# Latent attention with a ternary gated feed-forward on one core: fp16 scales from norms, score tiles in pairs

## What is computed

```python
c_kv, c_q = x @ w_dkv, x @ w_dq                       # ranks 64 and 192
k = concat([rope(x @ w_kr), c_kv @ w_uk])             # 16 heads of 64 + 128
q = concat([rope(c_q @ w_qr), c_q @ w_uq])
v = c_kv @ w_uv
out = softmax(q @ k.T / sqrt(192)) @ v @ w_o
x = layernorm(x + out)
x = layernorm(x + (silu(x @ w1q.T) * (x @ w3q.T)) @ w2q.T)   # ternary weights
```

## Time and profile before

| | us |
|---|---|
| median of 3 runs | 1019.66 |
| lowest, highest | 1019.26, 1024.77 |
| the profiled execution | 1020.77 |
| its span, first to last instruction | 1019.1 |
| mean granted TensorE clock | 0.974 |
| attention loops | some 128 to 451 and 608 to 933 |

### The profile page before, as it was taken

How to read it: one execution, slowest core, us unless ns; L and a number is a source line. 1 busy time by engine, 2 the same in 40 slices (tenths; PEclk the granted TensorE clock), 3 DMA queues, 4 the chain that set the end, 5 groups by cost and what they waited for, 6 DMA issues and landing times.

```text
span 1019.1 us, 17708 instructions
## 1 busy us (share of the span) xinstructions
PE 891.6 (87%) x5114; PEld 502.5 (49%) x5114; DVE 681.3 (67%) x1060; ACT 695.9 (68%) x1116; POOL 596.0 (58%) x401
## 2 busy tenths in 40 slices
PE   7888869998999999989889876999999999998985
PEld 3556534444444444448775642444444444444874
DVE  1877747777777777764458674777777777776455
ACT  2733668888888888881333466888888888887132
POOL 0008856767777767772341874776777776777134
PEclk9998979999999999999999897999999999999998
DMA  9734698887778877884510669897878877889301
GB/s 252 231 141 104 148 221 153 149 152 149 145 148 154 153 148 145 146 157 134 180 36 12 132 161 192 148 152 150 153 143 150 154 149 145 151 146 157 120 1 41
DMA packets 420800, 145.34 MB, mean 143 GB/s; under 512 B 405820, under 2 KB 413840, under 8 KB 419728
## 3 DMA queue, kind: packets, MB, share of 16 engines
q1 hardware_dynamic: 419584, 136.88, 67.5%
q10 hardware_dynamic: 592, 5.77, 1.4%
q0 software_dynamic: 576, 2.10, 0.6%
HBM read 23.85 MB, written 7.60 MB: 31 GB/s over the span
## 4 chain that ended last, share of the span: by engine, by line
PE 28%; ACT 25%; issue 20%; DVE 11%; POOL 9%; DMA 3%; ACTq 2%; SPq 1%; POOLq 0%; DVEq 0%
ACT probs L566 11%; ACT P_parts L451 8%; POOL P_parts L398 6%; PE Sb L1103 6%; DVE nmax L825 5%; PE Oa L1132 4%; ACT PT_hi L451 3%; PE Sa L1103 3%; DMA PT_dma<-P_parts 2%; ACT rden_row L451 2%; POOL g_lo L427 1%; DVE qmul L804 1%; PE Sa L1156 1%; PE Sb L1156 1%; DVE Q_parts L795 1%
## 5 line engine op out<-in xcount | busy, mean ns | idle before, releaser
L398 POOL TENSOR_TENSOR P_parts<-probs,P_parts 128x768 f16<-128x768 f32 x256 | 420.8, 1645 | 210.2 <-ACT P_parts L451 210.2
L451 ACT ACTIVATE P_parts<-probs 128x768 f16<-128x768 f32 x256 | 214.3, 838 | 17.0 <-DMA PT_dma<-P_parts 17.0
L566 ACT ACTIVATE probs<-Sa,nmax,limits 128x1024 f32<-128x1024 f32 x128 | 154.0, 1203 | 90.3 <-DVE nmax L828 90.1
L825 DVE TENSOR_REDUCE nmax<-Sb 128x1 f32<-128x1024 f32 x128 | 156.5, 1223 | 55.9 <-PE Sb L1103 55.7
L1103 PE MATMUL Sb<-K_hi,Q_parts 128*128 128x512 f16 x512 | 155.1, 385 | 43.6 <-ACT probs L566 42.8
L1103 PE MATMUL Sa<-K_hi,Q_parts 128*128 128x512 f16 x512 | 156.3, 388 | 34.8 <-ACT probs L566 34.7
L825 DVE TENSOR_REDUCE nmax<-Sa 128x1 f32<-128x1024 f32 x128 | 154.9, 1210 | 29.1 <-PE Sa L1103 29.1
L566 ACT ACTIVATE probs<-Sb,nmax,limits 128x1024 f32<-128x1024 f32 x128 | 154.3, 1205 | 1.5 <-DVE nmax L828 1.5
L1132 PE MATMUL Oa<-PT_dma,V_hi 128*64 128x512 f16 x768 | 132.4, 385 | 0.0
L1103 PEld LDWEIGHTS Sa<-K_hi,Q_parts 128*128 (+1 forms) x512 | 40.1, 99 | 118.7 <-issue 61.2
L371 POOL TENSOR_TENSOR turned<-qmul 128x1024 f32<-128x1024 f32 x16 | 40.1, 2528 | 93.5 <-DVE qmul L804 93.4
(11 more groups left out here) (300 smaller groups left out, 1536.6 us busy)
## 6 DMA issues: line engine op xcount, KB each, us to landing
Q_parts<-turned_parts SPq DMA_DIRECT2D x64, 128.0 KB, 2.4
TT<-ternary SPq DMA_DIRECT2D x2, 2304.0 KB, 9.7
Q_parts<-Q_parts SPq DMA_DIRECT2D x16, 256.0 KB, 2.9
PT_dma<-P_parts SPq DMA_TRANSPOSE x256, 3.6
ternary<-tern ACTq DMA_DIRECT2D x1, 2304.0 KB, 8.2
wo<-in_L_attn_w_o_dram SPq DMA_DIRECT2D x4, 512.0 KB, 8.6
xq<-in_L_attn_x_dram SPq DMA_DIRECT2D x2, 1024.0 KB, 12.1
wq_low<-Wq_lo ACTq DMA_DIRECT2D x1, 2048.0 KB, 12.7
```

The lines of the kernel that those rows point to most:

```text
L398: nc.gpsimd.tensor_tensor(P_parts[:, n % DEEP, 1, :], probs[n % DEEP][:, KP * P:S], P_parts[:, n % DEEP, 0, :], ALU.subtract).then_inc(par ...
L451: return nc.scalar.activation(o, i, ACT.Copy, scale=scale)
L566: nc.scalar.activation(probs[n % DEEP], SS[n % 2][:, :], ACT.Exp, bias=nmax[:, n % 4:n % 4 + 1], scale=score_down, accum_out=den[:, n // 8 ...
L825: nc.vector.tensor_reduce(nmax[:, n % 4:n % 4 + 1], SS[n % 2][:, :], AX.X, ALU.max, negate=True).then_inc(row_max, 1)
```

## The change

Three things are changed together.

**Scales from norms.** The fp16 scales no longer come from maxima of the finished keys and queries, but from bounds: the largest norm of a row of `x` (ScalarE squares eight slices with a running sum; VectorE, TensorE and VectorE take the largest), and maxima and norms of weights. Eleven small steps make the scales (one, a power of -1/2, on POOL), before keys and queries are copied out of PSUM; the scale is applied there, so keys, latent rows and queries are already scaled, and the later products need none. POOL rotates the key and takes its low part. POOL also makes `Wq_lo` of the rotary weights in the setup. SP issues the three stores of ScalarE, for batch 0 behind its loads. TensorE's transposes of `x` wait for `x` alone.

**Values by DMA.** `V_hi` and `V_lo` are DMA transposes of rows 64 to 127 of `K_hi` and `K_lo`. `turn_values`, `values_high` and the `V_lo` subtraction are gone.

**Tiles in pairs.** All four loops step by two tiles. TensorE: scores n + 2 and n + 3, then transposes n and n + 1, the row sums where due, then the values. ScalarE: exponent n + 2, high part of the transposes of n and n + 1, exponent n + 3, high casts n + 2 and n + 3. VectorE: both maxima, then the low part of the transposes. `row_out` moves from ScalarE to VectorE, and the high part of the output from VectorE's second product to a copy on POOL in `low_out`.

The core of the diff:

```diff
+                if b == 0:
+                    sp.wait_ge(wvo_sb, PAIRS)
+                    sp.dma_start(wvo_low, Wvo_lo_s[:, :, :].rearrange("p j d -> p (j d)").bitcast(F)).then_inc(wvo_out, 16)
+                    sp.wait_ge(ff_sb, 9)
+                    sp.dma_start(ternary, tern[:, :].bitcast(F)).then_inc(ff_out, 16)
+                    sp.wait_ge(prod_lo, PAIRS)
+                    sp.wait_ge(qr_lo, 4)
+                    sp.dma_start(wq_low, Wq_lo[:, :, :, :].rearrange("p h c m -> p (h c m)").bitcast(F)).then_inc(wq_out, 16)
...
+                sp.wait_ge(k_lat_hi, b + 1)
+                sp.dma_start_transpose(V_hi[:, :, :], K_hi[64:128, :]).then_inc(v_in, 16)
+                sp.wait_ge(k_lat_lo, b + 1)
+                sp.dma_start_transpose(V_lo[:, :, :], K_lo[64:128, :]).then_inc(v_in, 16)
...
+            for j in range(2):
+                for c in range(2):
+                    pool.wait_ge(qr_hi, 2 * j + c + 1)
+                    src = wqr[:, c, :].rearrange("p (g m two) -> p two g m", two=2, m=P)[:, j]
+                    nc.gpsimd.tensor_tensor(Wq_lo[:, j::4, c, :], src, Wq_hi[:, j::4, c, :].bitcast(F),
+                                            ALU.subtract).then_inc(qr_lo, 1)
...
+                pool.wait_ge(lim_step, b * LSTEPS + 5)
+                nc.gpsimd.tensor_tensor(pow_of, pow_in, minus_half[:, 0:2], ALU.pow).then_inc(lim_pow, 1)
+                pool.wait_ge(k_mul, b * 3 + 3)
+                nc.gpsimd.tensor_tensor(kmul[0:32, :], kmul[0:32, :], kturn[0:32, :], ALU.subtract).then_inc(k_rot, 1)
+                nc.gpsimd.tensor_tensor(kmul[32:64, :], kmul[32:64, :], kturn[32:64, :], ALU.add).then_inc(k_rot, 1)
+                pool.wait_ge(k_rot_hi, b + 1)
+                pool.wait_ge(k_rot, b * 2 + 2)
+                nc.gpsimd.tensor_tensor(K_lo[0:64, :], kmul[0:64, :], K_hi[0:64, :], ALU.subtract).then_inc(k_rot_lo, 1)
...
+                    hold(pool, out_ready, OUT0 + group + 1)
+                    nc.gpsimd.tensor_copy(O_parts[:, pair_row, cols], QO[:, pair_row + 1, cols]).then_inc(out_hi, 1)
                     hold(pool, out_hi, group + 1)
-                    hold(pool, out_ready, OUT0 + group + 1)
...
+                act_.wait_ge(y_ready, b * 2 + Y0)
+                for t in range(QT):
+                    nc.scalar.activation(qmul[:, t // 4, t % 4 * D:t % 4 * D + D], xq[:, t, :], ACT.Square,
+                                         accum_out=x_sums[:, t:t + 1]).then_inc(x_sq, 1)
...
                 act_.wait_ge(kv_ps, b + 1)
-                act_.wait_ge(wvo_out, 16)
-                copy(Kf[64:128, :], Sa[64:128, :]).then_inc(k_lat, 1)
+                act_.wait_ge(lim_step, b * LSTEPS + 7)
+                scaled(K_hi[64:128, :], Sa[64:128, :], k_up[64:128]).then_inc(k_lat_hi, 1)
...
-                copy(cq_hi[:, :], Sb[:, :], SCALE).then_inc(cq_hid, 1)
+                act_.wait_ge(lim_step, b * LSTEPS + 8)
+                scaled(cq_hi[:, :], Sb[:, :], cq_up).then_inc(cq_hid, 1)
                 act_.wait_ge(cqb_ps, b + 1)
                 for n in range(2):
-                    copy(cq_s[:, n * HALF:(n + 1) * HALF], TS[n][:, :], SCALE).then_inc(cq_hid, 1)
...
+                    scaled(cq_s[:, n * HALF:(n + 1) * HALF], TS[n][:, :], cq_up).then_inc(cq_hid, 1)
+                act_.wait_ge(k_rot, b * 2 + 2)
+                copy(K_hi[0:64, :], kmul[0:64, :]).then_inc(k_rot_hi, 1)
...
-                def row_out(group):
-                    act_.wait_ge(row_ps, group + 1)
-                    act_.wait_ge(out_ready, group + 1)
-                    copy(rden_row[:, :], Ob[:, :]).then_inc(row_ready, 1)
...
+                    for n in range(0, TILES, 2):
+                        ahead = not (last and n == TILES - 2)
+                        if ahead:
+                            exponent(t0 + n + 2, n + 2)
+                        transposed_high(t0 + n + 1, n + 1)
+                        if ahead:
+                            exponent(t0 + n + 3, n + 3)
+                            for m in (n + 2, n + 3):
+                                part_high(t0 + m, m, None if first and m < DEEP else 16 * (t0 // DEEP + m // DEEP))
...
+                act_.wait_ge(rope_sum, b * 2 * GROUPS + 2 * GROUPS)
+                exponent(b * PAIRS * TILES + 1, 1)
+                for n in range(2):
+                    part_high(b * PAIRS * TILES + n, n, None)
...
+                def row_out(group):
+                    dve.wait_ge(row_ps, group + 1)
+                    dve.wait_ge(out_ready, group + 1)
+                    nc.vector.tensor_copy(rden_row[:, :], Ob[:, :]).then_inc(row_ready, 1)
...
                     dve.wait_ge(row_ready, ROW0 + group + 1)
-                    nc.vector.scalar_tensor_tensor(O_parts[:, pair_row, h * HALF:(h + 1) * HALF], Oa[:, :], vscale[:, 3:4],
-                                                   rden_row[:, :], ALU.mult, ALU.mult).then_inc(out_hi, 1)
-                    nc.vector.scalar_tensor_tensor(QO[:, pair_row + 1, h * HALF:(h + 1) * HALF], Oa[:, :], vscale[:, 3:4],
+                    nc.vector.scalar_tensor_tensor(QO[:, pair_row + 1, h * HALF:(h + 1) * HALF], Oa[:, :], value_down,
                                                    rden_row[:, :], ALU.mult, ALU.mult).then_inc(out_ready, 1)
...
+                    for n in range(0, TILES, 2):
...
-                        if not (last and n >= TILES - 2):
+                        if not (last and n == TILES - 2):
                             maximum(t0 + n + 2, n + 2)
-                        if n % 2:
-                            transposed_low(pair * (TILES // 2) + n // 2, n)
+                            maximum(t0 + n + 3, n + 3)
+                        transposed_low(pair * (TILES // 2) + n // 2, n + 1)
+                        if n % 8 == 2 and not (first and n == 2):
+                            row_out(pair * 2 + n // 8 - 1)
...
+                pe.wait_ge(x_max, b + 1)
+                nc.tensor.transpose(Oa[0:1, 0:P], x_most, ident[:, :]).then_inc(x_row, 1)
...
+                project((SQ[2], SQ[3]), lambda kc: wdq[:, kc, :], 0)
+                pe.wait_ge(ones_ready, b + 1)
+                pe.wait_ge(w_max, b * 3 + 4)
+                pe.wait_ge(x_top, b + 1)
+                mm(Oa[:, P:P + 1], ones_b[0:1, :], sums[0:1, 7:8], start=True, stop=True)
+                mm(Oa[:, P + 1:P + 6], ones_b[:, :], limits[:, 1:6], start=True, stop=True).then_inc(sums_ps, 1)
+                project((SQ[2], SQ[3]), lambda kc: wdq[:, kc, :], 1).then_inc(cqa_ps, 1)
...
+                pe.wait_ge(k_mul, b * 3 + 3)
+                pe.wait_ge(k_lat_lo, b + 1)
...
+                query_terms(0, 2, range(5))
+                pe.wait_ge(lim_step, b * LSTEPS + 1)
...
-                        if g == 1 and j == 3:
-                            turn_values()
-                            pe.wait_ge(cq_lod, b * 4 + 4)
                         if g == GROUPS - 1 and j == 3:
-                            pe.wait_ge(k_lo, b + 1)
+                            pe.wait_ge(k_rot_lo, b + 1)
...
+                    for n in range(0, TILES, 2):
+                        for i in range(2):
+                            if not (last and n == TILES - 2):
+                                scores(t0 + n + i + 2, (n + i + 2) % TILES, p + (n + 2) // TILES)
+                        for i in range(2):
+                            transpose_probs(t0 + n + i, pair * (TILES // 2) + n // 2, n + i,
+                                            not (last and n == TILES - 2))
                         if first and n == 8:
+                            pe.wait_ge(v_in, b * 32 + 32)
                             pe.wait_ge(lat_lo, b * 4 * GROUPS + 4 * GROUPS)
...
                             if n % 8 == 2:
                                 sums_to_rows(pair * 2 + n // 8 - 1)
-                            if n % 2 == 1:
-                                for k in range(n % 8 - 1, n % 8 + 1):
-                                    values(pair * 2 + n // 8 - 1, 1 - n // 8, k)
+                            for k in range(n % 8, n % 8 + 2):
+                                values(pair * 2 + n // 8 - 1, 1 - n // 8, k)
```

262 lines of the change are left out of this document (101 added, 161 removed).

## The result

Median 962.46 us over four runs (961.35 to 965.38), against 1019.46 for the kernel before in the same comparison (1018.54 to 1024.77); ratio 0.943, 95% interval 0.939 to 0.947. The forecast was 957, range 932 to 990. The profiled execution took 965.38 us (span 963.7), 55.4 less than the profiled one of before.

The account below looks back on a forecast made before the run. A ring score, maximum, exponent, score beside a nearly full TensorE bounds the loops. From the profiled 1020.8 us: 28 half pairs -49, first half pairs -2, stages -11.5, end 0, giving 958.3, as median 957 us; range 932 to 990.

Parts of the forecast that it names:

- The two equations: Loop: two-tile round is second score group's start plus 3.24 us; round plus that start is 6.11; together 1.44 and 4.68.
- the ring: Attention loop: the cycle score, maximum, exponent, score over two PSUM tiles, taken as the limit beside a nearly full TensorE.
- ScalarE's 0.14 us: Loop: ScalarE's exponents and two casts end at 7.55 us, the next exponent is due at 7.69, so they fit by 0.14.
- Normalise: VectorE's output work: one instruction instead of two, 0.74 us less; ends 0.2 late, about 0.1 after the ring halves it.
- the cover of the transposes: Loop: the DMA transposes behind POOL's two output instructions land by 20.4 us, their buffer wanted at 21.1: covered by 0.7.
- high casts wait for PT_dma: Sign of a wrong forecast: ScalarE's high casts in the loop waiting for DMA transposes to land; none was expected.
- TensorE by starts: Loop: TensorE's floor per half pair counted from instruction starts, 18.6 us, instead of its busy row's 19.38.
- rotation starts 15.3 us behind the squares: Stage before the loops: query rotation starts 15.3 us after ScalarE's squares, at 69.2 us in batch 0, 552.4 in batch 1.
- TensorE's terms 1.9: Stage before the loops: TensorE's query terms, last part of the chain from squares to rotation, take 1.9 us.
- TensorE alone: Rival, loop: only TensorE bounds, half pair 18.6 us, 937 us in all; chance 0.15.
- The partial one: Rival, loop: a high cast waits 1 us for its buffer once per half pair, 20.2 us, 982 in all; chance 0.15.
- The ring of transposes: Rival, loop: transposes landing after 6.5 us instead of 3.6 return buffers late, making the kernel slower by 0.5%; chance 0.05.

Follow-up runs that it names:

- the kernel without the scaling: Changed kernel without VectorE's scaling of each maximum, the exponent taking constant bias and scale: 944.0 us, ratio 0.921, half pair 18.63 us.
- two normalises: Changed kernel with the output's high part made again by a second VectorE product, POOL's copy gone: 969.3 us, ratio 0.948, half pair 19.67 us.
- the second profile: Profiled execution of the changed kernel run again unaltered on another chip: median 961.9 us, ratio 0.941, half pair 19.19 us.
- the interleaved one: Changed kernel with the transposes of a round's first tile between its two score groups on TensorE: 957.2 us, ratio 0.936, half pair 18.80 us.

## Why the forecast held, and where it was off

**Loop, right.** 19.19 us for 19.3, and 52.5 us between the first and last marks of the two loops (30 half pairs) for 49 (28). The two equations and the 1.44 us from exponent to score group held to 0.02 us; the steady state they were solved for does not occur, only its mean. Moving one cast (20.65 for 20.9), adding one product (19.67 for 19.65) and taking 0.25 us from the ring (18.63 for 18.6 to 18.7) followed from them.

**ScalarE's 0.14 us, right as a mean outside the round of the row sums**, where 0.82 us are idle. The row copy cost nothing on either engine, so moving it is worth nothing in this order. On VectorE it took 0.68 (0.65).

**Normalise.** I took 0.1 us for being late. With one product VectorE ends at 280.06, when the maximum is due, so 0; the product that went saves 0.48.

**POOL, right; the cover of the transposes, wrong at single places.** The copy takes 0.60 (0.62). But the forecast named "high casts wait for PT_dma" as a sign of being wrong, and behind the start of each loop the profile has two: 1.40 us near the end and one of 0.2. "Landing varies by 0.1 us" was read in a quiet stretch (3.6 to 3.7 us in 262 to 400 us of before, but up to 5.0 ahead of it); in the changed kernel landings reach 5.5 to 5.9 us, and a cover of 0.7 us does not hold that. In four of the five profiles with a half pair of 19.2 us it costs 0.9 to 1.3 us in one half pair of one batch or of both, not 1 us in every one.

**TensorE by starts, right.** 18.6 us is the floor, and the kernel without the scaling reaches it with TensorE busy all the time. The Trainium skill, Perfetto Trace Analysis, section Identifying the Most-Contended Engine, judges TensorE's headroom by MFU and by the busy share of the weight loads. The weight loads fill 8.93 of 19.17 us, but with these matmuls the loop has 0.6 us left, not half. Here the share of the weight loads reads too much headroom.

**Stage, right in size at equal clock, not in its steps.** Forecast for batch 0, with the first half pair, -8.5: measured at the first mark -8.4 and -7.2 in two executions with the full clock, -0.75 in the profiled one. Batch 1: -5 forecast, -3.9 and -4.7 measured between the marks in the two profiles of the changed kernel. The step "rotation starts 15.3 us behind the squares" failed, at 17.6. Its term "TensorE's terms 1.9" was mis-sized: 5.7 us, for eight pairs of matmuls, the first of them at half pace behind an idle time that the kernel before does not have (there it is 0.25 us at most between query terms up to the rotation of batch 1). With two normalises the rotation of batch 0 starts at 69.27 us, as forecast (69.2), but by luck: its squares end at 52.0 instead of 53.9, and the 17.2 us behind them use this up. Smaller slips: a square took 0.40 to 0.44 us, inside the bounds, but the lower bound of 0.36 does not follow from the copy named (half of 0.59 and 0.2 are 0.50); POOL's part of `Wq_lo` took 2.1 us for each of four instead of 1.3, without effect on the time. The end, forecast 0, took 1.8 longer in this execution and 0.2 longer in the second profile (882.80 to 959.6).

**The 5 us between 957 and 962.** Forecast in all 62.5, measured 55.4 between the profiled executions: the loops gave 3.6 more than forecast with the 28 counted, the first mark 7.8 less, the stretch between the batches 1.1 less, the end 1.8 less. So the near hit of the whole is in part luck, a better loop against a later start. Most of the 7.8 is the setup of that execution: the transposes of `x` start 5.6 us later than in the one of before, which had the clock 1.00. Of eleven profiles with the changed setup two had that, one 0.93, three 0.86 and five 0.79. For the setup of before there are only two profiles, and whether the change makes the slower setup more frequent stays open.

**Rivals.** TensorE alone (18.6) is where the loop goes with 0.25 us less in the ring, not where it is. The partial one (20.2 in every half pair) exists as an event in single ones: 20.35 and 20.10 us in the second profile of the changed kernel, 20.28 in the interleaved one. The ring of transposes did not come: landings of 3.9 us in the median, not 6.5.
